# The first cross attention of a gated block on one core: heads of 64 rows in array halves, the maximum added by a selection product, the division moved behind the out projection

## The reference, cut to what matters

```python
x = x + tanh(g_xattn[0]) * xattn0(layernorm(x), ctx)   # 8 heads of 64
x = x + tanh(g_ffn[0])   * (self_attention(ln) + moe(ln))   # 16 heads of 8, 8 experts, top 2
x = x + tanh(g_xattn[1]) * xattn1(layernorm(x), ctx)   # 16 heads of 8
x = x + tanh(g_ffn[1])   * moe(layernorm(x))           # 8 experts, top 2
```

```python
q, k, v = split_heads(x @ Wq), split_heads(ctx @ Wk), split_heads(ctx @ Wv)
attn = softmax(q @ k.T * 64 ** -0.5)
out = merge_heads(attn @ v) @ Wo + bo
```

## Time and profile before

| | |
|---|---|
| median of three runs | 926.0 us (921.73 to 927.47) |
| profiled execution | 931.0 us from the first to the last instruction; the profile gives no other time for it |
| TensorE matmuls | 764.6 us busy, 82% |
| TensorE weight loads | 406.8 us, 44% |
| VectorE | 634.9 us, 68% |
| ScalarE | 353.3 us, 38% |
| GpSimd | 299.8 us, 32% |
| mean granted clock of TensorE | 0.861 of full |
| instructions | 13102 |

### The profile page before, as it was taken

How to read it: one execution, slowest core, us unless ns; L and a number is a source line. 1 busy time by engine, 2 the same in 40 slices (tenths; PEclk the granted TensorE clock), 3 DMA queues, 4 the chain that set the end, 5 groups by cost and what they waited for, 6 DMA issues and landing times.

```text
span 931.0 us, 13102 instructions
## 1 busy us (share of the span) xinstructions
PE 764.6 (82%) x5120; PEld 406.8 (44%) x5120; DVE 634.9 (68%) x1216; ACT 353.3 (38%) x444; POOL 299.8 (32%) x422
## 2 busy tenths in 40 slices
PE   4679798988999779987899799978898876786583
PEld 2355564644564245532464245534463433242231
DVE  0615577898655787678787988788556786964724
ACT  1324226214535234532545244632534244263060
POOL 5043442532244014332164135322244120333033
PEclk9879799998789788996899899996889778688587
DMA  5310300400303013030403023030503043023000
GB/s 146 76 35 15 69 10 10 101 11 6 74 15 57 11 54 77 12 57 6 113 18 60 9 66 71 21 42 8 128 1 54 1 108 78 2 68 57 2 1 12
DMA packets 64734, 40.95 MB, mean 44 GB/s; under 512 B 4912, under 2 KB 62776, under 8 KB 64664
## 3 DMA queue, kind: packets, MB, share of 16 engines
q1 hardware_dynamic: 64672, 40.12, 19.8%
HBM read 22.99 MB, written 17.10 MB: 43 GB/s over the span
## 4 chain that ended last, share of the span: by engine, by line
PE 52%; DVE 22%; DMA 12%; SPq 6%; ACT 4%; issue 2%; POOL 2%; POOLq 0%; DVEq 0%
PE psum L564 12%; DVE mx8B L903 12%; PE psum L651 8%; PE psum L571 6%; DMA q8B<-q_dB 6%; PE psum L607 5%; PE psum L639 3%; DVE mxA L826 3%; PE psum L545 3%; PE psum L555 2%; DMA qA<-mrow_d 2%; DMA k8F<-k_dF 2%; PE psum L614 2%; PE psum L620 2%; PE psum L550 1%
## 5 line engine op out<-in xcount | busy, mean ns | idle before, releaser
L903 DVE TENSOR_REDUCE mx8B<-psum 128x2 f32<-128x1024 f32 x128 | 149.9, 1214 | 42.0 <-PE psum L620 41.8
L564 PE MATMUL psum<-qA,cTX 97*128 97x256 f32 x512 | 146.7, 438 | 15.9 <-DMA qA<-mrow_d 12.8
L717 ACT ACTIVATE probB<-psum 128x1024 f32<-128x1024 f32 x128 | 125.7, 1026 | 53.9 <-PE psum L639 53.5
L951 POOL TENSOR_TENSOR half<-probX 128x512 f32<-128x512 f32 x64 | 81.5, 1274 | 165.7 <-ACT probX L704 164.9
L564 PEld LDWEIGHTS psum<-qA,cTX 97*128 97x128 f32 x512 | 106.1, 216 | 46.0 <-issue 21.8
L704 ACT ACTIVATE probX<-psum 128x1024 f32<-128x1024 f32 x64 | 65.6, 1024 | 158.4 <-PE psum L564 158.4
L620 PE MATMUL psum<-k8B,q8B 48*128 48x512 bf16 x256 | 60.8, 476 | 58.5 <-DVE mx8B L903 27.6
L717 ACT ACTIVATE probF<-psum 128x1024 f32<-128x1024 f32 x64 | 64.5, 1025 | 105.6 <-PE psum L639 104.0
L898 DVE TENSOR_REDUCE mx8F<-psum 128x4 f32<-128x1024 f32 x64 | 77.0, 1220 | 35.8 <-PE psum L614 35.7
L834 DVE RECIPROCAL rden<-psum 128x256 f32<-128x256 f32 x32 | 56.2, 1757 | 55.7 <-PE psum L575 55.6
L826 DVE TENSOR_REDUCE mxA<-psum 128x2 f32<-128x1024 f32 x64 | 76.9, 1216 | 13.5 <-PE psum L555 13.3
(11 more groups left out here) (191 smaller groups left out, 1129.7 us busy)
## 6 DMA issues: line engine op xcount, KB each, us to landing
k8B<-k_dK SPq DMA_DIRECT2D x16, 384.0 KB, 6.1
k_dK<-partsK SPq DMA_DIRECT2D x8, 384.0 KB, 4.0
q8F<-q_dF SPq DMA_DIRECT2D x16, 192.0 KB, 4.5
k8F<-k_dF SPq DMA_DIRECT2D x16, 192.0 KB, 4.9
q8B<-q_dB SPq DMA_DIRECT2D x16, 192.0 KB, 7.4
k_dK<-partsK SPq DMA_DIRECT2D x8, 256.0 KB, 4.0
cTX<-in_ctxT SPq DMA_DIRECT2D x8, 192.0 KB, 2.4
cTK<-in_ctxT SPq DMA_DIRECT2D x8, 192.0 KB, 2.5
```

Source lines behind the costliest of these rows:

```text
L564: last = mm(ps[:, c * SEQ:(c + 1) * SEQ], cT["X"][:, c * P:(c + 1) * P], qA[:, k, :], start=True, stop=True)
L717: nc.scalar.activation(prob[s][(units * b + k) % SLOTS[s]][:], ps, ACT.Exp, scale=float(D8) ** -0.5).then_inc(done["ACT"], 1)
L903: nc.vector.tensor_reduce(mx8[s][:, t, 2 * p:2 * p + 2], ps.rearrange("p (i n) -> p i n", i=2), AX.X, ALU.max, negate=True).then_inc(drain ...
L951: link("X", engine.tensor_tensor(half[:], p[:, 0:2 * SEQ], p[:, 2 * SEQ:], ALU.add))
```

## The change

- **Projections.** The folding goes. `qp` is one unit of four f32 products with 128 columns of weights, two heads on 128 partitions. `kp` is new: two units of two f32 products with 512 columns from the context. ScalarE copies each out twice, as bf16 and f32. `cb` goes.
- **Maximum.** `mx` has eight units, one for a head pair and a token half: two bf16 products of 64 rows, in the two row halves of the array. The maxima are transposed over all 128 columns (`mT`) and copied to `mrow` as bf16, on chip.
- **Scores.** A unit of `e` is one head pair and half of the keys. For each of two key blocks: two f32 products of 64 rows, one in each row half, and two bf16 products that add the maximum, with a selection matrix `pick` (made once on GpSimd) as weights. The way through DRAM (`mw`, `mr`) goes.
- **Sums.** GpSimd adds the key blocks of a head pair into `sums`. `dn` multiplies them with 32 columns of ones in four column strips, ScalarE copies the result, `dT` transposes it, and VectorE takes the reciprocals of 16 elements a token and multiplies them with the gate (`rX`).
- **Values and out projection.** `pv` has no `ones` product and is drained undivided by ScalarE. `out` has two units, one for each token half: eight f32 products of 64 rows in the row halves, head by head, 1024 columns. VectorE multiplies each head with its factor from `rX` (1024 elements), and GpSimd adds the eight heads and the residual in four additions (`xs`). F's layer norm now waits for `xs`.
- **Besides.** The first context load is issued ahead of the weights. B has six probability slots in place of seven. Some tiles of F and B now share space (`attT` with B's `xT`, `att` with `xmid` or B's `xh`), which adds waits.

```diff
-SLOTS = {"X": 4, "F": 4, "B": 7}
+SLOTS = {"X": 4, "F": 4, "B": 6}
...
     for k in range(2):
-        p.fill("ACT", 1, "X", "qp", b, k, 2.0, 2.05, [("DVE", "X", "ln", b, 0)],
+        p.fill("ACT", 1, "X", "kp", b, k, 1.8, 2.05, [("SP", "X", "ctx", b, 0)],
...
+    for k in range(UNITS):
+        g = UNITS * b + k - SLOTS["X"]
+        p.fill("ACT", 1, "X", "e", b, k, 1.2, 1.03, [("DVE", "X", "mT", b, 0)],
+               [("PE", "X", "pv", g // UNITS, g % UNITS // 2), ("POOL", "X", "e", g // UNITS, g % UNITS)])
+        p.job("POOL", "X", "e", b, k, 2.6 if k % 2 else 1.3, ("ACT", "X", "e", b, k), ("POOL", "X", "xs", b - 1, k // 4))
...
             load_x(0)
+            load_ctx("X", 0)
             for dst, src in first:
                 engine.dma_start(dst, src).then_inc(w_first, 16)
-            sp.wait_ge(c_set, 1)
-            load_ctx("X", 0)
...
                 elif name == "qp":
                     pe.wait_ge(*is_done(s, "ln", b))
-                    for j in range(4):
-                        last = mm(ps[0:CD, j * SEQ:(j + 1) * SEQ], wqk[:, 4 * k + j, :], xT[s][:], start=True, stop=True)
+                    for j in range(XH // 2):
+                        last = mm(ps[:, j * SEQ:(j + 1) * SEQ], wqx[:, j * P:(j + 1) * P], xT[s][:], start=True, stop=True)
+                elif name == "kp":
+                    pe.wait_ge(*after("X", "ctx", b))
+                    for j in range(2):
+                        last = mm(ps[:, j * KV:(j + 1) * KV], wkx[:, (2 * k + j) * P:(2 * k + j + 1) * P], cT["X"][:], start=True, stop=True)
...
+                    h, t = divmod(k, QT)
+                    for i in range(2):
+                        last = mm(ps[:, i * KV:(i + 1) * KV], qAb[64 * i:64 * i + 64, h, t * P:(t + 1) * P],
+                                  kAb[64 * i:64 * i + 64, h, :], start=True, stop=True)
...
                 elif name == "e":
-                    pe.wait_ge(*after("X", "mr", b))
-                    pe.wait_ge(*is_done("X", "qp", b, k // 4))
-                    for c in range(KV // P):
-                        last = mm(ps[:, c * SEQ:(c + 1) * SEQ], cT["X"][:, c * P:(c + 1) * P], qA[:, k, :], start=True, stop=True)
+                    pe.wait_ge(*is_done("X", "mT", b))
+                    pe.wait_ge(*is_done("X", "qp", b))
+                    pe.wait_ge(*is_done("X", "kp", b, k // 4))
+                    pe.wait_ge(picked, 1)
+                    h, f = divmod(k, 2)
+                    for c in range(2):
+                        for i in range(2):
+                            half_i = slice(64 * i, 64 * i + 64)
+                            mm(ps[:, 512 * i + SEQ * c:512 * i + SEQ * (c + 1)], kA[half_i, h, (2 * f + c) * P:(2 * f + c + 1) * P],
+                               qA[half_i, h, :], start=True, stop=False)
+                        for i in range(2):
+                            half_i = slice(64 * i, 64 * i + 64)
+                            last = mm(ps[:, 512 * i + SEQ * c:512 * i + SEQ * (c + 1)], pick[half_i, h, :], mrow[half_i, :],
+                                      start=False, stop=True)
...
-                    pe.wait_ge(*up_to("X", "psum", b, 2 * k + 2))
-                    for i in range(2):
-                        last = mm(ps[64 * i:64 * i + 64, SEQ:2 * SEQ], ones[:], psum_k[(2 * k + i) % 4][:], start=True, stop=True)
+                elif name == "dn":
+                    pe.wait_ge(*after("X", "psum", b))
+                    for g in range(2):
+                        for j in range(4):
+                            last = mm(ps[32 * j:32 * j + 32, g * SEQ:(g + 1) * SEQ], ones[:], sums[:, 2 * g + j // 2, j % 2, :],
+                                      start=True, stop=True, tile_position=(0, 32 * j))
+                elif name == "dT":
+                    pe.wait_ge(*is_done("X", "dn", b))
+                    for n in range(2 * QT):
+                        last = transpose(ps[:, n * P:(n + 1) * P], dS[:, n * P:(n + 1) * P], ident[:])
                 elif name == "out":
...
-                    for t in range(QT):
-                        for j in range(XH // 2):
-                            last = mm(ps[:, t * P:(t + 1) * P], oTX[:, j, t * P:(t + 1) * P], wox[:, j, :],
-                                      start=(j == 0), stop=(j == XH // 2 - 1))
+                    for j in range(XH // 2):
+                        for i in range(2):
+                            half_i = slice(64 * i, 64 * i + 64)
+                            last = mm(ps[:, 512 * i + j * P:512 * i + (j + 1) * P], oX[half_i, j, k * P:(k + 1) * P], wox[half_i, j, :],
+                                      start=True, stop=True)
...
+                elif name == "xs":
+                    pool.wait_ge(*is_done("X", "out", b, k))
+                    q = prodX[k]
+                    link("X", engine.tensor_tensor(q[:, 0:512], q[:, 0:512], q[:, 512:1024], ALU.add))
+                    link("X", engine.tensor_tensor(q[:, 0:256], q[:, 0:256], q[:, 256:512], ALU.add))
+                    link("X", engine.tensor_tensor(q[:, 0:128], q[:, 0:128], q[:, 128:256], ALU.add))
+                    pool.wait_ge(*after("X", "xb", b))
+                    pool.wait_ge(*after("F", "xh", b - 1))
+                    pool.wait_ge(*after("F", "fin", b - 1))
+                    engine.tensor_tensor(x1["F"][:, k, :], q[:, 0:128], xb["X"][:, k, :], ALU.add).then_inc(S["X"]["xs"], 1)
```

More of the change, by code:

```diff
@@ L303, in build @@
         iota = sb("iota", [P, NE])
[L304 to L305 removed]
+        ones = sb("ones", [P, 32])
+        pick = sb("pick", [P, XH // 2, P], BF16)
+        wqx = sb("wqx", [P, XH * XD])
+        wkx = sb("wkx", [CD, XH * XD])
         wvx = sb("wvx", [CD, XH * XD])
@@ L338, in build @@
         xT = per("XFBC", "xT", [P, SEQ])
-        qA = sb("qA", [CD + 1, XH, SEQ])
-        qAb = sb("qAb", [CD, XH, SEQ], BF16)
-        cTb = sb("cTb", [CD, KV], BF16)
+        qA = sb("qA", [P, XH // 2, SEQ])
+        qAb = sb("qAb", [P, XH // 2, SEQ], BF16)
+        kA = sb("kA", [P, XH // 2, KV])
+        kAb = sb("kAb", [P, XH // 2, KV], BF16)
         vX = sb("vX", [P, KV // P, XH * XD])
-        mxA = sb("mxA", [P, QT, XH])
-        mrow = sb("mrow", [XH, SEQ])
+        mxA = sb("mxA", [P, QT, P])
+        mrow = sb("mrow", [P, SEQ], BF16)
         prob = {s: [sb(f"prob{s}{n}", [P, 4 * SEQ]) for n in range(SLOTS[s])] for s in "XFB"}
[L346 to L351, removed]
+        sums = sb("sums", [P, XH // 2, 2, SEQ])
+        oX = sb("oX", [P, XH // 2, SEQ])
+        rX = sb("rX", [P, QT, XH])
+        dS = sums[:, 0].rearrange("p i n -> p (i n)")
+        prodX = [sums[:, 2 * n:2 * n + 2].rearrange("p h i n -> p (h i n)") for n in range(QT)]
         width = {"F": 2 * SEQ, "B": SEQ, "K": KV}
@@ L589, in _ @@
                     pe.wait_ge(*after("K", "ctx", b))
-                    last = mm(ps[:, 0:KV], wk8["B"][:], cT["K"][0:CD, :], start=True, stop=True)
+                    last = mm(ps[:, 0:KV], wk8["B"][:], cT["K"][:], start=True, stop=True)
                 elif name in ("v8", "vv"):
@@ L777, in _ @@
                     elif s == "F":
-                        dve.wait_ge(*is_done("X", "out", b))
+                        dve.wait_ge(*after("X", "xs", b))
                     elif s == "B":
@@ L919, in link @@
                 pool.wait_ge(S[s]["pch"], links[s])
-            for tile in (cT["X"], ones, cT["K"], k8["F"], k8["B"], v8["F"], v8["B"]):
+            engine.memset(nhalf[:], -0.5).then_inc(c_set, 1)
+            engine.memset(mxA[:], 0.0).then_inc(c_set, 1)
+            engine.memset(ones[:], 1.0).then_inc(c_set, 1)
+            for tile in (k8["F"], k8["B"], v8["F"], v8["B"]):
                 engine.memset(tile[:], 1.0).then_inc(c_set, 1)
-            engine.memset(nhalf[:], -0.5)
             pool.wait_ge(w_first, W_FIRST)
@@ L938, in _ @@
                         pool.wait_ge(*after("X", "xin", b))
-                        pool.wait_ge(*is_done("X", "out", b - 1))
+                        pool.wait_ge(*after("X", "xs", b - 1))
                     else:
```

203 lines of the change are left out of this document (103 added, 100 removed).

## The result

Four runs of the changed kernel gave 938.12 to 958.18 us, median 948.2; four of the kernel before 916.1 to 927.47, median 923.9. The ratio is 1.0187, 95% interval 1.0096 to 1.0279. The forecast was 874, with a range of 848 to 908. The two longest runs of the changed kernel, the profiled one (span 956.2) among them, lie over 1.5% above its fastest, so the ratio, and every median and difference further down, goes by the other runs alone: 940.9 us for the changed kernel. Some 15 us of the spans and stretches shown next are therefore that execution's own.

A forecast was written before the change was run, and what follows sets the result against it. TensorE's matmul work was taken as the largest lever, not the only one. TensorE -40, start -7, later waits -6, cold units -5, GpSimd path +6 gave -52 on 931.0: 879, or 874 for the median; range 848 to 908.

The forecast's parts named there:

- A: Rival: f32 row halves run one after the other, a scores unit costs 2.24 us, total about 946 us; chance 7%.
- Scores unit: First cross attention on TensorE: a unit falls from 1.92 to 1.27 us, 5.2 us less a batch.
- Maximum: First attention's maximum products: a pair falls from 0.54 to 0.32 us in row halves, 1.8 us less a batch.
- Denominators: Softmax sums on TensorE: the ones units go, 1.7 us less; dn at 1.00 and dT at 0.44 add 1.4.
- Out projection: First attention's out on TensorE: 1.80 us becomes 2.4 with 32 records of 64 rows, 0.6 more a batch.
- Sum on TensorE: All matmul terms of the first attention together: 5.0 us less a batch, 40 us in eight.
- Start: Before the first scores unit: 7 us less, first unit near 45 us; removing the folding gains nothing.
- Path through GpSimd: Last value product to F's norm grows about 7 us; shows for first and last batch, 6 us added in all.
- Six slots: B's probability slots, six for seven: still hold two units ahead, counted at nothing.
- From 603 to 612.5 everything waits: Reading of the kernel before's profile: in this stretch (us) everything waits for the stacked queries of B.
- B: Rival: GpSimd's addition gates each batch, 7 us shows in each, 50 us come back, 924 us; chance 6%.
- C: Rival: gain half hidden by the query load and VectorE stage kept in each period, TensorE clock lower, 900 us; chance 25%.

The follow-up runs named there:

- e1_own_place: Changed kernel with B's attention result and its transpose moved from B's shared tiles to free places in oU: 886.8 us, ratio 0.957 to the kernel before.
- e2_sharing_alone: Kernel before with only B's two shared tiles and their waits added, first attention as before: 990.8 us, ratio 1.076.
- e5_order_kept: e1_own_place with the planner still told of the shared tiles, so engine orders are those of the changed kernel: 956.6 us, ratio 1.030 to the kernel before.
- e6_one_row_half: e1_own_place with both products of each scores pair on rows 0 to 63: 983.4 us, ratio 1.062 to the kernel before.
- e7_no_head_sum: e1_own_place with the first three of GpSimd's four xs additions left out: 884.7 us, ratio 0.956 to the kernel before.
- e3_six_slots: Kernel before with six slots for B's probabilities in place of seven: 933.0 us, ratio 1.0087.

## Why the prediction was wrong

**The step that failed** is one that I left out. The prediction goes through the tiles of B in one sentence (the seventh slot, "I count nothing") and passes over the shared tiles, though the section on the change says that they add waits, and the full diff has `plan_norm` of B follow `out8` of the batch before in place of `qk`. In its sum the sharing is a term of nothing, without a reason. What to apply stands in the section on the kernel before: a piece that waits holds up all that is behind it on its engine. The trace before had the answer: B's queries at 355.01, the out projection of the batch before at 445.96. A wait that reverses two things 91 us apart needs a price. Measured, it is 54 us (e1_own_place against the changed kernel) or 64 (e2_sharing_alone against before), more than the whole forecast gain of 52. How it costs that I would not have foreseen: through the order planned around it, not as waiting (e5_order_kept). The prediction's last sentence names just this, an order that leaves TensorE idle, as what would make it wrong "above all", but gives it no chance and no price: its 0.07 for slower is all A's. The price lay in the kernels. `schedule()` ends with the time that it plans for each piece (`OVER`), and the latest is 890 us in the kernel before, 906 in the changed one, 829 in e1_own_place and 995 in e2_sharing_alone; measured are 924, 941, 887 and 991. The plan is off by 34 to 58 us in three of the four, but under the same planned costs it ranks all four as measured, and it needs no chip.

**Scores unit**, 1.27 forecast: 1.09 to 1.29, by its neighbours (last section). Right, and e6_one_row_half shows that the halves are the reason.

**Maximum**, 0.32: right or better, 0.22 to 0.32 from fill to fill at full clock. **Denominators**: `dn` 1.00 as forecast, `dT` 0.44 to 0.59.

**Out projection**, 2.4 forecast within 1.8 to 3.6. In the kernel after, 16 records at 115.90 and 16 at 117.11:

```profile
115.90 1.16 PE L596 MATMUL psum<-wox,oX 64*128 64x128 f32 x16
116.89 0.38 PE L549 MATMUL psum<-kAb,qAb 64*128 64x512 bf16 x2
117.11 1.06 PE L596 MATMUL psum<-wox,oX 64*128 64x128 f32 x16
118.10 1.12 PE L543 MATMUL psum<-wvx,cTX 96*128 96x512 f32 x2
```

0.99 each, 2.0 in all: twice the weight loads of the earlier trace rows in nearly the same time. The 3.4 us estimated from what the Trainium skill says in "TensorE: Matmul & The Clock Gate", section on LDWEIGHTS, does not occur; what the Trainium skill says in "TensorEngine Tiling (Array Packing)", Key Properties, that different tiles load in parallel, is what this trace shows for two row halves: a load every 0.06 us in place of 0.11.

**Sum on TensorE**, 40 us: 54 in e1_own_place (764.6 to 710.4), a slightly higher clock included. But the span fell by 45 us (931.0 to 886.0), so TensorE stands idle 9 us longer, where the prediction's terms have it 7 us shorter. No run splits these 16 us, or the 13 between 886.8 and the forecast. **Start**: the first scores unit begins at 34.8 us, not at 45. The prediction has the K product keep its place ahead of X's queries and so counts nothing for the folding. In the new order X's keys, values and queries fill the time from 10.47 to 21.4 us and the K product comes behind them, at 22.12; the first maxima start at 23.1 and not at 31.0. `kp` took 1.9 us in the median, not 1.72.

**Path through GpSimd**, 6 us: nothing measurable (e7_no_head_sum). **Six slots**, 0: just under 1%, measured on the kernel before (e3_six_slots).

**Two readings.** "From 603 to 612.5 everything waits" is too strong: the earlier trace rows have TensorE busy for 6.81 and VectorE for 6.36 of those 9.5 us. And the period of 99 us in the kernel before is the shortest of its kind: its loads of B's queries stand at 297.40, 400.93, 505.85, 604.79 and 712.55 us, 99 to 108 apart.

**Rivals.** A and B are out. C (the gain half hidden behind the load of B's queries) held in part even with the tiles apart: the loads of B's queries stand at 259.10, 357.34 and 458.84 us in e1_own_place, a period of 98 to 102 us where I forecast 92, TensorE waits 32.9 us for them where it was 26.0 before, and 886.8 lies between the forecast and C's 900. The mean clock did not fall, though (0.871 for 0.861). The reason was not that the load can't be hidden: with a longer cost for it in the plan, TensorE waits for none of these loads and the same instructions take 846.

## What to carry to other kernels

A tile that is shared to save memory is an edge between two batches: look up in the trace before how far apart the two uses stand and in which order, and find a place whose readers are long done (here a buffer of the same stream, free in just that stretch). Where a planner with fixed costs writes the order, each edit draws a new order, and that alone moved the instructions of e1_own_place between 794 and 957 us; so look first at the end time that the plan itself gives, compare kernels under several plans, and check the planned costs of transfers against the trace. A wait can be removed on the chip without gain as long as the order still honours it.

## What was not expected of the hardware

No row of the kernel before had an f32 product in row halves. Two of them, in rows 0 to 63 and 64 to 127, take 0.43 to 0.54 us together for 256 columns at full clock, against 0.87 to 0.97 when both use the same rows. Their f32 weight loads overlap as well: the 32 loads of `out`, each of 128 columns, pass in 2.0 us, where 16 loads of the earlier trace rows take 1.80.

The upper values have a cause that the traces show. A unit of scores or of `out` takes 0.10 us more for each neighbour in TensorE's order that isn't in row halves too. In e1_own_place at full clock a unit of scores takes 1.09 us with both neighbours in row halves, 1.19 with one and 1.28 with none; a unit of `out` takes 0.89, 0.99 and 1.09. A maximum takes 0.22 us, or 0.32 when the unit behind it isn't in row halves. So an order that keeps such units next to each other could be worth up to 0.2 us a unit, an estimate from these times; no run tried it.
